# A gated cross-attention block with a quantised convolutional feed-forward: one tile of each batch quantised on GpSimd, fewer chunks convolved apart, new instruction lists

## The reference

```python
x = x + tanh(g_xattn) * attention(layernorm(x), ctx, ctx)      # 16 heads of 16, biases on q, k, v, o
x = x + tanh(g_ffn) * ffn(layernorm(x))
def ffn(x):
    h = bit_linear(x, w1)                    # 256 -> 1024
    h = depthwise_conv1d(h, conv_w, conv_b)  # 3 taps along the tokens, one filter per channel
    return bit_linear(silu(h), w2)           # 1024 -> 256
def bit_linear(x, w):
    scale = 127 / clip(max(|x|) over the channels of a token, 1e-5)
    xq = clip(round(x * scale), -128, 127) / scale
    wscale = 1 / clip(mean(|w|), 1e-5)
    wq = clip(round(w * wscale), -1, 1) / wscale
    return xq @ wq.T
```

## Time and profile before

| what | value |
|---|---|
| median of 3 runs | 168.48 us (168.1 to 170.43) |
| profiled execution | 169.36 us |
| its span, first to last instruction | 167.2 us |
| busy: PE, DVE, ACT, POOL | 143.8, 135.2, 112.3, 88.3 us |
| granted TensorE clock, mean | 0.98 |

### The profile page before, as it was taken

The page is one execution under the profiler, slowest core; times in us unless marked ns, Lnnn a source line. Parts: engine busy times, 40 slices in busy tenths (PEclk is TensorE's granted clock), DMA queues, the critical chain, the costliest instruction groups (busy, mean ns, idle before and its releaser), DMA issues.

```text
span 167.2 us, 3548 instructions
## 1 busy us (share of the span) xinstructions
PE 143.8 (86%) x1314; PEld 79.1 (47%) x1324; DVE 135.2 (81%) x240; ACT 112.3 (67%) x176; POOL 88.3 (53%) x88
## 2 busy tenths in 40 slices
PE   7839979999799999999999796999565999984792
PEld 3238435424565336652576242568333353743461
DVE  6455999961953669995837999999999969989993
ACT  0304598779616488899999997999498586652220
POOL 0204899999910542398370089882979943200330
...
GB/s 134 269 386 395 339 6 0 4 0 0 0 0 2 4 0 0 0 0 4 4 2 0 4 0 2 0 6 0 0 125 0 4 4 0 67 67 0 3 79 169
DMA packets 5919, 8.68 MB, mean 52 GB/s; under 512 B 528, under 2 KB 4880, under 8 KB 5648
## 3 DMA queue, kind: packets, MB, share of 16 engines
...
HBM read 6.38 MB, written 2.10 MB: 51 GB/s over the span
## 4 chain that ended last, share of the span: by engine, by line
PE 29%; DVE 24%; ACT 24%; issue 15%; DMA 5%; ACTq 1%; DVEq 0%
ACT hid L1181 6%; DMA w_attn<-attn_w 5%; PE ps L445 5%; DVE u L790 4%; DVE mx L720 4%; ACT probs L1120 3%; PE ps L311 3%; DVE hid_q L860 3%; DVE hmax L812 3%; PE ps L348 3%; PE ps L507 2%; ACT side L1169 2%; ACT xn L1079 2%; PE ps L397 2%; DVE top L768 2%
## 5 line engine op out<-in xcount | busy, mean ns | idle before, releaser
L790 DVE TENSOR_TENSOR u<-ps,deq_b 128x512 f32<-128x512 f32 x32 | 20.2, 679 | 4.1 <-PE ps L436 3.6
L1433 POOL TENSOR_TENSOR hid<-hid,side 128x512 f32<-128x512 f32 x12 | 15.6, 1305 | 8.8 <-ACT side L1166 8.8
L720 DVE TENSOR_REDUCE mx<-ps 128x16 f32<-128x1024 f32 x16 | 18.8, 1212 | 1.4 <-PE ps L321 1.4
L445 PE MATMUL ps<-u,conv_w 32*32 32x512 f32 (+1 forms) x576 | 18.5, 544 | 0.9 <-ACT hid L1188 0.7
L1120 ACT ACTIVATE probs<-ps 128x1024 f32<-128x1024 f32 x16 | 15.4, 1029 | 5.6 <-PE ps L348 5.5
L1445 POOL TENSOR_TENSOR x_s<-x_s,grown 128x512 f32<-128x512 f32 x6 | 7.6, 1277 | 21.1 <-ACT grown L1198 21.1
L860 DVE TENSOR_TENSOR hid_q<-hid,ps 128x1024 f16<-128x1024 f32 x16 | 18.6, 1215 | 0.0
L436 PE MATMUL ps<-xqT,w1q 128*128 128x512 bf16 x57 | 15.3, 397 | 3.6 <-ACT xqT L1139 2.9
L1440 POOL TENSOR_TENSOR hid<-hid,side 128x512 f32<-128x512 f32 x12 | 15.5, 1305 | 4.2 <-ACT side L1169 3.8
L507 PE MATMUL ps<-w2q,hid_q 128*128 128x256 f16 x128 | 15.6, 273 | 1.3 <-DVE hid_q L860 1.3
L311 PE MATMUL ps<-xT,w_attn 128*128 128x512 f32 x32 | 15.0, 601 | 0.9 <-DVE mx L720 0.9
...
## 6 DMA issues: line engine op xcount, KB each, us to landing
...
out<-x_s SPq DMA_DIRECT2D x6, 256.0 KB, 2.1
hid<-w_t SPq DMA_DIRECT2D x1, 1024.0 KB, 18.4
hid<-w_t ACTq DMA_DIRECT2D x1, 1024.0 KB, 12.3
...
w_attn<-attn_w SPq DMA_DIRECT2D x1, 256.0 KB, 5.7
```

Source lines behind the costliest of these rows:

```text
L445: last = nc.tensor.matmul(ps[ROWS * g:ROWS * g + ROWS, banks[s], first:first + n], conv_w[rg, 4 * q + s, tap, :], u[rg, 4 * q + s, first + ...
L720: nc.vector.tensor_reduce(mx[:, b % 2, k, 0:HEADS], ps[:, bank:bank + 2, :].rearrange("p c (h k) -> p (c h) k", k=KEYS), AX.X, ALU.max).th ...
L790: nc.vector.tensor_tensor(u[:, f, 1:N + 1], ps[:, bank, :], deq1_b[:, b % 2, :], ALU.mult).then_inc(u_ready.sem, 1)
L1433: nc.gpsimd.tensor_tensor(dst, dst, side[:, m % TMPS, 0, :], ALU.add).then_inc(left_ready.sem, 1)
```

## The change

- `APART` holds batches 0 and 1 only. Batch 2 has all its eight chunks on PE, with a second `convolve(2, 1)`; its twelve taps on ACT and eight additions on POOL go.
- `TURNED` holds all four batches: the last tile (tokens 384 to 511) of each is quantised by POOL's new `quantise_hidden`. GpSimd reads the scale from SBUF, so ACT copies it out of PSUM first (`take_scale2`), into the place of the key weights, which nothing reads after `keys`. The scale of that tile is put into the next bank.
- The key slice of the weights takes the place of the query slice on SP's queue, and the reverse on ACT's.
- The small DVE instructions on 128x4 or 128x2 elements with constant operands (`tensor_scalar`) become `tensor_tensor` or `scalar_tensor_tensor` with constants read from SBUF. `var` and `minus_mean` have a signal each, and DVE's `norm` subtracts the mean itself.
- The lists of PE, DVE, ACT and POOL are written anew.

```diff
-APART = frozenset([0, 1, 2])
+APART = frozenset([0, 1])
+TURNED = frozenset([0, 1, 2, 3])
...
+        scale2_col = w_attn[:, 1, 0, 0:P]
...
-            sp.dma_start(w_attn[:, 0], attn_w[:, 0]).then_inc(wq_in, 16)
+            sp.dma_start(w_attn[:, 1], attn_w[:, 1]).then_inc(wk_in, 16)
...
-                    last = nc.tensor.transpose(ps[:, bank, k * P:(k + 1) * P],
+                    at = bank + (b in TURNED and k == T - 1)
+                    last = nc.tensor.transpose(ps[:, at, k * P:(k + 1) * P],
                                                qscale2[:, b % 2, k:k + 1].to_broadcast([P, P]), idf[:])
...
-                nc.vector.tensor_scalar(var[:, b], mv[:, b, :, 1], LN_EPS, None, ALU.add).then_inc(var_ready.sem, 1)
+                nc.vector.tensor_tensor(var[:, b], mv[:, b, :, 1], eps[:].to_broadcast([P, T]),
+                                        ALU.add).then_inc(var_ready.sem, 1)
...
-                nc.vector.tensor_scalar(step1[:, a], top1[:, a], CLIP, 1.0 / QMAX, ALU.max,
-                                        ALU.mult).then_inc(step1_ready.sem, 1)
+                nc.vector.scalar_tensor_tensor(out=step1[:, a], in0=top1[:, a], scalar=CLIP,
+                                               in1=step_of[:, 0:1].to_broadcast([P, T]), op0=ALU.max,
+                                               op1=ALU.mult).then_inc(step1_ready.sem, 1)
...
+            def take_scale2(b, bank):
+                act.wait_ge(*(scale2_half_ps(0, 1) if b == SPLIT else scale2_ps(b)))
+                n = nth(b, TURNED)
+                if n:
+                    act.wait_ge(*hq_turned(n - 1))
+                nc.scalar.copy(scale2_col, ps[:, bank, (T - 1) * P:T * P]).then_inc(col_ready.sem, 1)
...
-            act.dma_start(w_attn[:, 1], attn_w[:, 1]).then_inc(wk_in, 16)
+            act.dma_start(w_attn[:, 0], attn_w[:, 0]).then_inc(wq_in, 16)
...
+            def quantise_hidden(b, k):
+                pool.wait_ge(*col_ready(nth(b, TURNED)))
+                if b:
+                    pool.wait_ge(*f2_ps(b - 1, k // 2))
+                tile = slice(k * P, (k + 1) * P)
+                nc.gpsimd.tensor_tensor(
+                    hid_q[:, :, tile].rearrange("p (q i) n -> p q i n", i=2),
+                    hid[:, b % 2, 0:FP, tile, :].rearrange("p q n i -> p q i n"),
+                    scale2_col.unsqueeze(1).unsqueeze(1).to_broadcast([P, FP, 2, P]),
+                    ALU.mult).then_inc(hq_turned.sem, 1)
```

More of the change, by code:

```diff
@@ new lines, in _ @@
+            denominators(0, 0, 2, mx_ready(1, 1))
+            values(0, 1, 3, mx_ready(1, 1))
+            denominators(0, 1, 2)
+            scores(2, 0, 6, mx_ready(1, 2))
+            turn_max(1, 3, o_ready(0, 1))
+            turn_den(0, 2, den_ready(0))
+            turn_xn(3, 0, 5, qT_ready(2, 1))
+            scores(2, 1, 0, mx_ready(1, 3))
+            scores_t(1, 0, 6, mx_ready(2, 0))
+            scores_t(1, 1, 2, rden_ready(0), neg_ready(1))
+            scores_t(1, 2, 4, o_ready(0, 0), xT_ready(3, 0))
@@ new lines, in _ @@
+            project_q(3, 1, 6, p_ready(2, 1))
+            spread_deq1(0, 7, p_ready(2, 1))
+            denominators(2, 0, 2, p_ready(2, 2))
+            turn_xq(0, 3, p_ready(2, 2))
+            scores(3, 0, 4, p_ready(2, 3))
+            scores(3, 1, 0, qT_ready(3, 0), x1_ready(1, 1))
+            denominators(2, 1, 2)
+            values(2, 0, 3, xqT_ready(0))
+            values(2, 1, 6, qT_ready(3, 1))
+            hidden(0, 0, 7, deq1_ready(0))
+            hidden(0, 1, 3, o_ready(2, 0))
@@ L1044, in _ @@
+            quantise_hidden(3, 2, 0)
+            residual2(3, 0, 1)
+            residual2(3, 1, 0)
         @block.scalar
@@ L1465, in _ @@
             spread_keys(0)
+            spread_keys(1)
             root(1)
```

748 lines of the change are left out of this document (363 added, 385 removed).

## The result

| | before | after |
|---|---|---|
| median of the runs | 168.93 us (168.1 to 170.43) | 159.63 us (159.01 to 160.77) |
| ratio | | 0.945 (0.936 to 0.954) |
| profiled execution, its span | 169.36, 167.2 us | 159.01, 157.1 us |
| second group of runs | 169.83 us (168.34 to 171.29) | 160.34 us (159.74 to 161.72), ratio 0.944 (0.939 to 0.950) |

The changed kernel is 5.5% faster. Medians are of all executions; ratios, with 95% intervals, leave out those that fell in the slower of the chip's two states. The forecast was 165.1 with a range down to 161.5, so the sign was right and the size was not: the gain was 3.4 us in the sum and is 9.3 to 9.5 us on the chip.

The account below looks back on a forecast made before the run. A chain bounds the start, PE the attention stages, DVE the feed-forward. Pieces of 27.0, 48.4, 17.4 and DVE's remainder gave a span of 163.8 against 167.2; 3.4 off 168.48 gave 165.1 us, range 161.5 to 169.2.

Parts of the forecast that it names:

- Piece 1: Start up to turn_max of batch 0: ends at 27.0 us, bounds 26.1 and 28.7; rival of no gain there, 0.12.
- The keys' chain: From keys at 7.9 through transposes, project_q, value_rows and DVE's maxima and statistics: reaches turn_max at 26.1 us.
- The two gates: Two chains ahead of turn_max: from the keys, 26.1 or 27.6 us by clock; through ACT's weight_sum and norm(1), 27.0.
- Piece 2: turn_max to first hidden of batch 0, PE bound: 43.5 us of calls plus 11% gives 48.4; late-hidden rival 0.10.
- Piece 3: First hidden of batch 0 to the end of convolve(0, 0): 16.6 us on PE plus 5% gives 17.4.
- Piece 4: After convolve(0, 0) to the span's end: 0.5 us, DVE work 64.4, idle 3.8, then 2.25 behind DVE's last instruction.
- The second convolution absorbed: Batch 2's added convolution, 3.40 us on PE, hides beside DVE; rival of PE as the bound, 168.5 us, 0.11.
- DVE bounds there: In the feed-forward DVE is the bound, busy 71.12 of 74.95 us before, with PE 13.5 us free.
- GpSimd's tile: POOL's quantise_hidden takes 2.6 us each, saves DVE 4.6 over four; the last is level with its cover at the end.
- The small instructions: New forms on DVE still wait for GpSimd, 3.0 us kept; rival of no waits 162.1 us, 0.32 with smaller idle time.
- gain nothing: The new small-instruction forms on DVE bring no gain: all 3.0 us of waits for GpSimd stay.
- three marked-up terms: Additions to counted work: 11% for bubbles in attention, 5% up to convolve(0, 0), and 3.8 us of DVE idle time.

Follow-up runs that it names:

- project_twice: Changed kernel with both project_q calls of batch 2 computed twice on PE: 163.49 us, one execution.
- lists_only: Changed kernel with its lists and two batches apart, but old weight queues, old small instructions and all tiles on DVE: 167.19 us, ratio 0.985.
- before_apart2: Kernel before with batch 2 convolved wholly on PE by a second convolve(2, 1), the other lists as they were: 172.68 us, ratio 1.021.
- conv2_short: Changed kernel without batch 2's second convolution but for one matmul of two columns: 160.54 us, beside 160.34 for the changed kernel in the same group.
- tile_twice: Changed kernel with each of POOL's four tiles computed twice, the second waiting for the first: 163.65 us, ratio 0.970.
- forms_only: Kernel before with only the small DVE instructions changed to read constants from SBUF: 169.77 us, ratio 0.998.
- no_swap: Changed kernel with the old queues of the key and query weights: 162.85 us, ratio 0.965.
- swap_only: Kernel before with only the queues of the key and query weights exchanged: 167.57 us, ratio 0.988.
- second run of after: Changed kernel run once more, unchanged, in the second group of runs: 160.34 us, six executions.
- old_forms: Changed kernel with the small DVE instructions as tensor_scalar again: 162.53 us, ratio 0.958.
- no_turned: Changed kernel with all tiles quantised on DVE, without the four ACT copies and four POOL tiles: 163.72 us, ratio 0.968.
- old_forms_fill: Changed kernel with the old small instructions plus two matmuls that feed nothing in PE's idle spells before the last second calls: 161.51 us, ratio 0.950.

## Why the prediction was right or wrong

The sum gave a span of 163.8 where 157.1 was measured, 6.7 too much. By its own pieces:

- **Piece 1** said 27.0 and it is 26.99, in part by luck. The keys' chain, reckoned at 26.1, ends 0.8 later, 0.6 of it because the keys start at 8.54 and not at 7.9. The two gates that it named are level: ACT's copy for `turn_max` ends at 26.94 and PE's work ahead of it at 26.99. What the table adds is that the piece is keys plus 18.45 us, and that the keys wait for the context, which lands 6.2 to 7.6 us after its issue and so moves them from 7.95 to 9.44 between runs. The swap was worth more than a start that comes 1.7 earlier, because of the clock (below).
- **Piece 2** is the step that failed most: 45.12 for 48.4, **3.3 us**. The count of calls was right, 43.5 us. The error was the mark-up of 11% for bubbles, 4.9 us, where 1.6 were measured: I took the difference between 34.5 and 38.35 in the old lists as a share of the calls and carried it over in proportion. It wasn't one. Part of it was PE's idle time, 1.63 us, which belonged to the order of the old list; the new list has 0.40. What is left over the count is 2.2 of busy time before and 1.2 after. Calls that are added fill gaps as well as make them: project_twice added 3.4 and cost 2.54.
- **Piece 3** said 17.4 for 16.70, **0.7**: a mark-up of the same kind, at 5%, on a stretch in which PE was busy for all of it.
- **Piece 4** said 71.0 for 68.29, **2.7**. DVE's work was 63.1 and not 64.4, 0.6 of it because the small instructions wait 2.4 and not 3.0; the rest isn't traced to instructions. Its idle time was 2.4 and not 3.8. I had kept the idle time of before in size, though its rows (waits for PE at a `hidden`, for ACT at the half maxima) belonged to places in the old list. In lists_only the waits for a `hidden` and a convolution (0.90 and 0.41) are gone and that at the half maxima is 0.30 for 0.77; before_apart2 has one of 5.28. So these waits are a property of the order.
- **The second convolution absorbed** was right, and conv2_short shows it: leaving it out changes nothing. In the old lists the same work costs 3.1 to 3.6 (before_apart2), so "DVE bounds there" was the right reason only because the new list has DVE's supply ahead of it; before_apart2 puts the convolution ahead of the `hidden` calls that DVE needs next.
- **GpSimd's tile** was 2.42 for 2.6, and the gain of all four 4.0 for 4.6. The forecast let only the last tile reach the end; tile_twice shows that the others do too when they are longer, over the additions behind them. Nor was the last tile level with its cover: at 2.42 it ended 1.0 ahead.
- **The small instructions** do still wait for GpSimd in the new form: 1.06 at 147.51, 0.53 at 102.61. The Trainium skill's rule ("SBUF — State Buffer", section "SBUF: two separate sides") is that whichever of the two starts first holds the shared ports for its whole instruction. It agrees where DVE starts clearly second: 102.83 in forms_only, 147.51 here. Where both start within 0.01 us it doesn't tell the forms apart, 0.13 against 1.30, and the measurement decides. So "gain nothing" was wrong in the new lists: the form is worth 1.17 us at that one place, of the 1.65 between first `hidden` and tiles, in all thirteen profiles. At the end the shorter `deq2` lets `step2` start ahead of GpSimd's addition, for 0.3 us; that part is argued from the two traces. In the old lists the same edit gave nothing, and there no `deq2` starts level with a GpSimd addition.
- **The clock** was missing from the sum. I had used 0.65 at 11 to 15 only as a bound of piece 1. Before and no_swap run the keys after 3.28 and 3.53 us of idle PE, and the granted clock then falls to its lower level (1.2 of 2.4 GHz) for part of the matmuls behind them. It doesn't in every execution: in lists_only, after 3.01 us of idle, the keys took 1.97. After 0.73 us it didn't fall in the changed kernel, but a short wait ahead of the keys is no guarantee. In swap_only, where PE also waits 2.16 ahead of `value_rows` at 13.15, it was 0.68 at 15 to 19, and in the second run of after, behind waits of 0.61, 0.96 and 0.73, it was 0.70 at 24 to 28.
- **The range** was too narrow at the low end. It let the small instructions go with most of the better start, but gave the three marked-up terms (4.9, 0.8 and 3.8) no lower bound. Without any of the three the span would have been 154.3 in place of 163.8, and the measured 157.1 lies between.

The parts don't add up one by one. Undone alone, queues, forms and tiles cost 3.4 + 2.2 + 4.0 = 9.6 us; undone together (lists_only) they cost 6.8. With intervals of some 2 us on each term, that gap of 2.8 isn't clear of noise. The table tells more. Its spans exceed that of after by 5.2, 3.7 and 5.0, together 13.9, and lists_only by 7.8. Between first `hidden` and tiles the three add up to 4.67 and lists_only has 4.34, so they nearly do add up. Of the 6.1 between the sums, 1.6 are the later landing of the context in old_forms and no_turned, which moves from run to run, 1.3 the clock behind the keys in no_swap, and 2.7 the clock at the last matmuls of no_swap and old_forms. The profiled execution of lists_only kept 1.00, as two of its four did, and no_turned kept 0.998 or more in all four. For old_forms the drop is shown by old_forms_fill; for no_swap it is read from one profile.

Open: why a new small instruction that starts level with GpSimd's runs beside it and an old one doesn't; and why the clock falls at the end in some executions of one and the same kernel and not in others.
